# All four hat loads in one queue, and a new order of parts on every engine

## The reference, cut to what matters

```python
# L0: conditional convolution: 1x1 (256->64), 3x3 (64->64), 1x1 (64->256); each weight is a
#     mix of 8 experts, and the mix comes from the means of the input
cw = jnp.einsum('be,eoikl->boikl', rw, w)
# L1: in-projection, depthwise conv, tokens permuted per head, selective scan, tokens put back,
#     gate, out-projection
dA = jnp.exp(dt[:, :, None, :] * A[None, :, :, None]); dB = dt[:, :, None, :] * Bt
# L2: 1x1, offsets by a 3x3, deformable 3x3 (bilinear), 1x1
val = v00 * wy0 * wx0 + v01 * wy0 * wx1 + v10 * wy1 * wx0 + v11 * wy1 * wx1
# L3: 1x1, 3x3, 1x1, each followed by (y + 1) ** 2
```

## Time and profile before

| | |
|---|---|
| median of 3 runs | 1134.95 us (1133.67 to 1144.43) |
| profiled execution | 1137.99 us |
| its span, first to last instruction | 1135.9 us |
| mean granted clock of PE | 0.87 of full speed |
| busy: PE, DVE, ACT, POOL | 949.5, 766.0, 552.7, 355.2 us |
| DMA | 123.31 MB, mean 109 GB/s |

### The profile page before, as it was taken

One profiled execution on the slowest core, in us unless ns is written; L12 is line 12 of the kernel. 1 busy time (PEld: TensorE's weight loads), 2 busy tenths in 40 slices (PEclk: granted clock), 3 DMA queues, 4 the chain that ended last, 5 costly groups with the idle time before them and its releaser, 6 DMA issues.

```text
span 1135.9 us, 19270 instructions
## 1 busy us (share of the span) xinstructions
PE 949.5 (84%) x7176; PEld 651.0 (57%) x7176; DVE 766.0 (67%) x2047; ACT 552.7 (49%) x1155; POOL 355.2 (31%) x320
## 2 busy tenths in 40 slices
PE   3779798998889898989889898989898998867534
PEld 2546476665656565756566665656575665545222
DVE  2658375868778795959596876968595958555232
ACT  1134353737365564647383736546464737261502
POOL 2012415243233414152433323250515233233100
PEclk9688769899999898989898996979898989886756
DMA  9011251424425161615243442516161524334160
GB/s 221 16 33 29 60 170 41 149 89 119 136 79 179 55 194 52 201 36 173 80 150 101 119 136 75 180 54 194 48 189 50 152 85 131 114 97 143 27 170 15
DMA packets 116546, 123.31 MB, mean 109 GB/s; under 512 B 64802, under 2 KB 99750, under 8 KB 116454
## 3 DMA queue, kind: packets, MB, share of 16 engines
q1 hardware_dynamic: 103492, 83.33, 26.0%
q10 hardware_dynamic: 6818, 25.04, 6.4%
q0 software_dynamic: 6144, 13.71, 4.0%
HBM read 84.32 MB, written 37.73 MB: 107 GB/s over the span
## 4 chain that ended last, share of the span: by engine, by line
PE 52%; DVE 15%; DMA 10%; issue 9%; ACT 6%; POOL 5%; SPq 1%; ACTq 1%; POOLq 0%; DVEq 0%
PE ps L620 49%; DMA y_turned<-b_yt 6%; POOL b_yp L1234 4%; DMA b_yp<-y_turned,b_to 4%; DVE x L1280 2%; ACT c_pad L955 2%; DVE y L1277 1%; PE ps L834 1%; DVE st L1307 1%; SPq L1795 1%; DVE b_adt L1272 1%; ACT y L955 1%; DVE b_yt L1283 1%; DVE y L1280 1%; PE ps L798 1%
## 5 line engine op out<-in xcount | busy, mean ns | idle before, releaser
L1234 POOL DMA_INDIRECT b_yp<-y_turned,b_to x64 | 82.5, 1289 | 311.0 <-DMA y_turned<-b_yt 296.4
L620 PE MATMUL ps<-y,inw 128*128 128x392 f32 x384 | 141.4, 506 | 0.2 <-DVE y L1277 0.2
L1186 POOL TENSOR_TENSOR rs<-ve,root 128x4 f32<-128x4 f32 x64 | 65.8, 1029 | 219.4 <-DVE ve L1276 219.0
L620 PE MATMUL ps<-c_w,c_zt 126*64 126x196 f32 x896 | 109.2, 400 | 21.5 <-DMA c_zt<-z_turned 18.0
L1307 DVE BATCH_NORM_STATS2 st<-x 128x6 f32<-128x196 f32 x256 | 73.5, 349 | 76.8 <-POOL x L1186 68.0
L620 PE MATMUL ps<-w,a_S 128*32 128x384 f32 (+2 forms) x1280 | 91.9, 431 | 26.2 <-DVE a_S L1280 24.1
L620 PEld LDWEIGHTS ps<-c_w,c_zt 126*64 126x64 f32 x896 | 73.7, 168 | 53.7 <-issue 36.4
L1272 DVE TENSOR_TENSOR c_w<-c_w,c_hat 126x1176 f32<-126x1176 f32 (+1 forms) x64 | 97.6, 1580 | 8.9 <-DMA c_w<-hat_turned 8.9
L955 ACT ACTIVATE x<-ps,cvec 128x392 f32<-128x392 f32 x32 | 18.7, 587 | 167.1 <-PE ps L620 167.1
L620 PEld LDWEIGHTS ps<-y,inw 128*128 128x128 f32 x384 | 69.3, 193 | 39.5 <-issue 3.0
L1208 POOL DMA_INDIRECT x_turned<-b_xt,b_to x64 | 63.6, 994 | 55.1 <-DVE b_xt L1283 43.1
(11 more groups left out here) (201 smaller groups left out, 2087.4 us busy)
## 6 DMA issues: line engine op xcount, KB each, us to landing
z_turned<-c_z SPq DMA_DIRECT2D x32, 441.0 KB
c_zt<-z_turned SPq DMA_DIRECT2D x16, 882.0 KB
c_w<-hat_turned ACTq DMA_DIRECT2D x16, 771.8 KB
c_w<-hat_turned SPq DMA_DIRECT2D x16, 771.8 KB
c_w<-hat_turned ACTq DMA_DIRECT2D x16, 578.8 KB
c_w<-hat_turned SPq DMA_DIRECT2D x16, 578.8 KB
b_xp<-x_turned SPq DMA_DIRECT2D x32, 222.0 KB
x<-in_x SPq DMA_DIRECT2D x32, 196.0 KB, 2.7
```

The source lines that it names most:

```text
L620: return nc.tensor.matmul(o, l, r, start=start, stop=stop)
L1186: return nc.gpsimd.tensor_tensor(out=o, in0=x, in1=y, op=op)
L1234: nc.gpsimd.indirect_dma_start(out=YP[:, m, h].rearrange("p b d -> p (b d)"), out_offset=None, in_=y_dram[g % 2], in_offset=bass.IndirectO ...
```

## The change: where the loads are issued, and the order

`load_hats` is called by SP alone. The three steps of d2 on SP are now: h = 0 of both images, then the turned z, then h = 1 of both images. ACT has no load of hats left. The wait for the previous group's product (`filled(... "acc", g - 1 ...)`, which says that `c_w` and `c_zt` may be overwritten) stands once, ahead of the first load; those of the ACT loads and of the z load, which came after it, go.

```diff
-        def load_hats(eng, b, h, g):
+        def load_hats(sp, b, h, g):
             if h == 0:
-                if g:
-                    filled(eng, "acc", g - 1, H)
+                if b == 0 and g:
+                    filled(sp, "acc", g - 1, H)
                 if first(g):
-                    eng.wait_ge(ranked, 1)
-                eng.wait_ge(*hat_out[b].at(g))
+                    sp.wait_ge(ranked, 1)
+                sp.wait_ge(*hat_out[b].at(g))
...
             def d2(i, part, g):            # scalar
-                if i == 0:
-                    load_hats(act, 1, part, g)
                 if i == 3:
...
             def d2(i, part, g):            # sync
                 if i == 0:
-                    load_hats(sp, 0, part, g)
-                else:
-                    if g:
-                        filled(sp, "acc", g - 1, H)
+                    load_hats(sp, part, 0, g)
+                if i == 2:
+                    load_hats(sp, part, 1, g)
+                if i == 1:
                     for m in range(2):
                         sp.wait_ge(*z_out[m].at(g))
```

All numbers of `PLAN` and `FROM` change. `FROM` had nearly equal steps with small departures, larger for the last groups; now each stage's step is the same for all groups:

```diff
 FROM = {
...
-    "d2": (84039, 144936, 205833, 266730, 327619, 388516, 449461, 510310, 571207, 632104, 693001, 753898,
-        814807, 876052, 936109, 1023526),
+    "d2": (0, 60897, 121794, 182691, 243588, 304485, 365382, 426279, 487176, 548073, 608970, 669867, 730764,
+        791661, 852558, 913455),
```

More of the change, by code:

```diff
@@ L236 @@
-    "once": (84039,),
+    "n0": (0, 60897, 121794, 182691, 243588, 304485, 365382, 426279, 487176, 548073, 608970, 669867, 730764,
+        791661, 852558, 913455),
+    "c0": (0, 60897, 121794, 182691, 243588, 304485, 365382, 426279, 487176, 548073, 608970, 669867, 730764,
+        791661, 852558, 913455),
+    "n1": (0, 60897, 121794, 182691, 243588, 304485, 365382, 426279, 487176, 548073, 608970, 669867, 730764,
+        791661, 852558, 913455),
+    "s1": (0, 60897, 121794, 182691, 243588, 304485, 365382, 426279, 487176, 548073, 608970, 669867, 730764,
+        791661, 852558, 913455),
@@ L237 @@
+    "once": (0,),
 }
@@ L250 @@
-        (297390,),
-        (300106, 300746, 302963),
-        (61968, 106689, 119060),
+        (22381,),
+        (76793, 78031, 78111, 79976, 83244, 83245, 85186, 99088, 135839, 137433),
+        (138927,),
+        (141971, 141971, 143541, 144175, 144175, 145654),
+        (146794, 147644, 148266, 165302),
+        (199905, 199920, 199920, 199920, 201161, 201161, 202172, 203783, 204981, 205022),
+        (208542, 210199, 227235, 228574),
+        (254393,),
+        (258681, 259241, 259484, 259484, 259484, 259484, 259601, 259691, 260006, 260192, 260192),
@@ new lines @@
+        (98287, 103270),
+        (114367, 121114, 121910, 123364),
+        (150074, 151324, 158851),
+        (158992, 160867, 162127, 162127, 163220, 163942, 164195, 170223, 175264, 175264, 177562, 177562, 177562,
+        177562, 180190, 180190, 180277, 183422),
+        (209119, 211359),
+        (212397, 213770, 218562),
+        (219542, 219977, 219977, 220198, 220198),
+        (267792, 268119, 268119, 268265, 277531, 279459),
+        (279459, 279742, 280213),
+        (320138, 320939),
```

118 lines of the change are left out of this document (47 added, 71 removed), and 4 rows, old and new, of the table PARTS.

## The result

| | before | after |
|---|---|---|
| median of the runs side by side | 1137.99 us (4 runs) | 1089.2 us (4 runs) |
| ratio, 95% interval | | 0.9545 (0.9465 to 0.9626) |
| profiled execution, its span | 1137.99, 1135.9 us | 1081.92, 1079.7 us |
| granted clock of PE | 0.870 | 0.901 |
| start to the load of `b_xp` for group 2 | 201.05 us | 200.35 us |

The changed kernel is 4.5% faster; I had forecast no change, 1137 us. Some executions of any of these kernels run at a lower granted clock and are longer; the ratios leave them out, but the profiled executions of two later runs, e17 and e18, are of this kind. Of the 56.2 us between the spans of the two profiled executions 45.3 lie in the 13 periods in the middle, 3.5 in each, and 10.2 at the end. (The profiled execution after is 7 us shorter than the median of its kernel.)

What follows compares the result with a forecast made beforehand. PE was the first suspect, its wait at the transposes passing from the DMA gather to DVE. Per period -0.3 + 0.7 = +0.4, times 15 is +6; end -4: 1138.0 to 1140.0, median 3.0 lower, 1137 us; range 1108 to 1166.

Steps and rivals of the forecast that it cites:

- the sum at an equal clock: Per period, without clock effects: 0.3 us won up to the out-projection, what follows even.
- From the out-projection to c1w: The 5.0 us from n2's statistics to c1w, nearly all a DVE, POOL and ACT chain, stays: 0.
- From the y products to the out-projection: PE waits 0.6 us for DVE at the transposes; out-projection 15.7 us behind the y products, 17.1 before: -1.4.
- the wait for ACT's copies: DVE, ahead of the transposes, waits for the projections' copies, moved behind a table load: 1.2 us, between 0 and 2.
- Up to the end of the y products: The 1x1 on d_h,d3w (0.93 us) now stands ahead, plus 0.2 for small waits: +1.1 us per period.
- The clock: Half clock around the transposes remains and falls on out-projection and hats' parts: +0.7 us per period, between -2.3 and +2.
- a sign of being wrong: Forecast wrong if the clock around the transposes is not what it was, or if DVE idles for c_w.
- The y store: One load less ahead of it on the DMA engines: it lands, and the gather of b_yp starts, 3 us earlier.
- The end: Last group: z ahead of h = 1 lets three of seven parts run early: -4 us, between 0 and -8.
- the pause goes and the clock stays: Faster rival, chance 0.17: nothing holds the transposes, PE runs through, the half-clock stretch goes too; 1108 us.
- The lock: Faster rival, chance 0.06: POOL's product stands elsewhere, DVE regains 0.84 us per period from their shared ports; 1124 us.
- The gate: Slower rival, chance 0.35: PE from the transposes waits for DVE's fourth hats' product and the last-issued load; +1.3 per period, 1156 us.

Runs made afterwards that it cites:

- e17: Kernel before with L3's end moved forward and L0's branch early, queues as before, no fillers: 1155.83 us, ratio 1.0079.
- e18: e10 with all four hats' loads in SP's queue: 1080.66 us, ratio 0.9462.
- e10: Kernel before, old order and queues, with 11 useless matmuls (fillers) per group in PE's four larger waits: 1109.12 us, ratio 0.9736.
- e14: e12 with L0's end put back (3x3 behind the out-projection, small product right ahead of the third mix): 1096.77 us, ratio 0.9658.
- e16: e12 with L3's end put back (1x1 behind the y products, DVE's two sums between hats' products and gate): 1096.94 us, ratio 0.9665.
- e12: e11 with more useless matmuls (12, 4 and 3) in PE's waits of the last group: 1058.12 us, ratio 0.9265.
- e1: Kernel before with only the loads changed: all four hats' loads in SP's queue around z, old order: 1111.63 us, ratio 0.98.
- e13: e12 with the old loads (hat 1 in ACT's queue, z behind hat 0 in SP's): 1067.6 us, ratio 0.9372.
- e2: Changed kernel with the old loads (hat 1 in ACT's queue), new order kept: 1101.65 us, ratio 0.9725.
- e6: Kernel before with L3's end moved forward on PE, ACT and DVE, as in the new order: 1149.48 us, ratio 1.0089.
- e9: Kernel before with L0's 3x3 and the small product for the third mix moved early, queues as before: 1158.78 us, ratio 1.0195.
- e11: Changed kernel with useless matmuls per group, 2 ahead of c1w's y and 3 ahead of c_pad: 1056.38 us, ratio 0.929.
- e15: e12 with the statistics of n0 put back on PE and DVE: 1056.47 us, ratio 0.9281.
- e8: Changed kernel with four useless matmuls per group ahead of PE's wait for c_pad: 1071.69 us, ratio 0.9388.

## Why the prediction was wrong

**The failed step is the sum at an equal clock**: -0.3 us a period up to the out-projection "and what follows is even". Measured with the clock held up it is -3.8 to -4.0, of which up to 1.3 may be e10's fillers, so -2.5 at least.

- *From the out-projection to c1w*, predicted 0, measured -1.4 without fillers and -2.0 with them. I took the 5.0 us from the statistics to c1w for a chain through DVE, POOL and ACT. In the kernel before, PE's queue held the small product and the third mix ahead of c1w, and PE waited there for DVE, 4.3 and 14.8 us in the 13 periods, as its list of waits says:

```profile
PE ps L620 <- DVE a_S L1280: 14.8, 12, 1.9
...
PE ps L620 <- DVE a_m L1276: 4.3, 11, 0.8
```

  I read the 5.0 us off two starts and asked only how long it was, not what stood in it. e14 puts this back and loses it.
- *From the y products to the out-projection*, predicted -1.4 (15.7 against 17.1), measured -3.2. The way on DVE was right: the statistics read 11.2 us behind the y products (11.8 predicted), the wait for ACT's copies 16.2 us in 13 periods, 1.2 each, as predicted, the out-projection at 15.0 in this period (15.7). The old order was mis-sized. I took off 2.3 us for the clock, and filled, at 0.99, it still needs 18.1: from the transposes to the out-projection it is 6.2 us where it was 7.6, and the transposes come 1.0 later. PE still waits 1.5 us a period there for the gather (19.0 in the 13), and 32 products of hats follow between the last transposes and the out-projection: in the kernel before `b_res` was ready at 617.35 (616.02 + 1.33) and PE came to it at 619.96. The new order has eight there and the rest behind, and the 3x3 stands ahead of the transposes, where PE would wait anyway. 1.3 of the 3.2 come with the new queues alone (18.1 to 16.8 in e18), for which I had counted nothing.
- *Up to the end of the y products*, predicted +1.1, measured +1.2. The number is right, the reason not: in e16 the 1x1 on `d_h,d3w`, 0.93 of my 1.1, is back behind the y products, and the stretch from c1w to the end of the next y products is as long (31.2 us against 31.3), since PE then waits for `b_re` (8.7 us in the 13 periods, against 2.8 in e12). What sets this stretch stays open.
- *The clock*, +0.7, came about otherwise than I had said. I let the thin stretch around the transposes stay and its low clock fall on dearer work; instead the low clock there went (0.66 to 1.00), which I had named as a sign of being wrong, and the one behind the out-projection stayed. A low clock costs the old kernel 1.6 us a period, up to 2.9 if the fillers cost what they may, and the new one some 1.9: between +0.3 and -1.0. That this lies near my sum is luck.
- *The y store*, 3 us earlier: 2.4 in e1, from which the middle gains at least 1.0 a period in the old order (e18). I counted nothing of it, since DVE would end the wait. In the traces of the new order that is nearly right (e13: ten of 13 periods the same). In the ratios it isn't shown to be: e2 is 1.8 points behind the changed kernel (intervals that don't overlap) and e13 about 1 behind e12 (intervals that do); the few periods that still wait show a part of that, the rest is open.
- *The end*, -4, measured -10.2. From the last load of `b_xp` to the store of the hats it is 4.0 shorter (71.8 to 67.8), which is the order (71.8 in e1, 67.5 in e2), and from there 6.2 (61.8 to 55.6). z is issued 7.6 us behind that store where it was 16.0, and PE waits 10.3 us for it and later 4.2 for a product of hats, instead of 18.0. The queues do this in the old order by themselves (55.3 in e1); in the new order they are worth 1.2 (56.8 in e2). Why z came so late in the kernel before stays open: e10 has the old queues and the old order too, and issues it 7.8 us behind the store.

Of the rivals, *the pause goes and the clock stays* had the right side and more than half the gain (1108 us), for the wrong reason: the pause went, but the 1.2 GHz time it set free was not most of what the period gained. *The lock*: some of DVE's long steps did get shorter, `x<-d_o` from 944 to 627 ns (24.5 to 16.3 us in the 13 periods) and the norms' `y` from 461 to 376 ns. The Trainium skill, SBUF — State Buffer, "The single rule", says that the pair of ports which DVE and POOL share is an exclusive lock; the row of e16 that took 1.26 us beside POOL's sum, and 0.63 without it, agrees. What it was worth alone was not measured; e6 shortened DVE's work in the old order and was slower. *The gate* did not close in the changed kernel: DVE waited for `c_w` 0.2 us in the 13 periods. e16 shows how near it was: with L3's end behind the products DVE waits for the fourth load for some 1.5 us in most periods.

## What to carry to other kernels

Ask of a stretch between two instructions not how long it is but what stands in it on the engine's own queue: work for another branch ahead of the instruction that matters is on the path, with its waits. An order is worth what its pieces are worth together; L0's end and L3's end each made the old order slower (e6, e9) and were each missed in the new one (e14, e16). Split a gain into clock and chain only with the clock held equal: of 45 us, 29 looked like the clock's, and with the clock equal in both at least two thirds of the gain a period were left. And when a change has two parts, hold the clock up for all four combinations before you name the one that did it.

## What the runs showed that I had not expected

Fillers in PE's waits make this kernel faster. Five in each group, 2.7 us of PE's time a period, take the changed kernel from 0.9545 to 0.929 of the time before, and e11 at 1056.38 us (with e12 and e15, which can't be told from it) is the fastest version that I ran. They raised the granted clock of the whole from 0.901 to 0.941, in waits of 1.1 and 1.4 us. Four in one place only, ahead of `c_pad` (e8), gave 0.9388. What they would do on a chip whose other cores are at work was not tried.
